# Cross attention: row maximum in bank-sized parts, and a new order of work in the four engine lists of a step

## The reference

```python
kvx = jnp.einsum('bsi,oi->bso', cond, w_kv_x)          # cond: (16, 1601, 256)
kx, vx = jnp.split(kvx, 2, axis=-1)                    # 8 groups of 128
kx = _ln(kx.reshape(b, sc, g, d), kxln_w, kxln_b)      # layer norm of each key
xout = _gqa(qx, kx, vx)                                # softmax(q k / sqrt(128)) v
cat = jnp.concatenate([core, xout], axis=-1)
catq = _div_clamp_fp8(cat, proj_smooth)                # rounding to fp8
```

## Time and profile before

| | before |
|---|---|
| median of 3 runs | 2706.87 us |
| profiled execution | 2704.8 us |
| its span, first to last instruction | 2703.0 us |
| TensorE busy | 2299.4 us (85%) |
| VectorE busy | 2032.5 us (75%) |
| ScalarE busy | 1556.2 us (58%) |
| GpSimd busy | 1472.4 us (54%) |
| mean granted TensorE clock | 0.937 |

### The profile page before, as it was taken

How to read it: one execution, slowest core, us unless ns; L and a number is a source line. 1 busy time by engine, 2 the same in 40 slices (tenths; PEclk the granted TensorE clock), 3 DMA queues, 4 the chain that set the end, 5 groups by cost and what they waited for, 6 DMA issues and landing times. The chain is left out here.

```text
span 2703.0 us, 49677 instructions
## 1 busy us (share of the span) xinstructions
PE 2299.4 (85%) x18258; PEld 1833.9 (68%) x18258; DVE 2032.5 (75%) x4418; ACT 1556.2 (58%) x3133; POOL 1472.4 (54%) x1529
## 2 busy tenths in 40 slices
PE   2888737999999999999999999999999999675566
PEld 1555525877777878787778777777787877553334
DVE  8988845777878787877877787787878777468763
ACT  5767615666666666666666666666666666321211
POOL 3343366666667666676767666666766654250000
PEclk8887759999999999999999999999999999887778
DMA  2010131000110110011010100111011000073100
GB/s 109 40 47 24 47 131 57 27 32 27 52 33 26 34 47 32 27 39 46 26 33 34 45 27 32 35 44 33 34 33 39 20 9 1 28 264 94 35 12 8
DMA packets 74623, 119.41 MB, mean 44 GB/s; under 512 B 21184, under 2 KB 56592, under 8 KB 73360
## 3 DMA queue, kind: packets, MB, share of 16 engines
q1 hardware_dynamic: 74384, 116.23, 12.6%
HBM read 94.20 MB, written 22.02 MB: 43 GB/s over the span
## 5 line engine op out<-in xcount | busy, mean ns | idle before, releaser
L75 PE MATMUL x_kc<-x_wk,x_ctxT 128*128 128x256 f16 x4992 | 624.0, 274 | 49.5 <-POOL x_ctxT L1015 36.7
L1037 POOL TENSOR_TENSOR x_kT<-x_kf,x_kT 128x512 f16<-128x512 f32 (+1 forms) x448 | 625.5, 1396 | 37.3
L75 PE MATMUL x_ox<-x_ctxp,x_pt 128*128 128x256 f16 x4992 | 619.0, 273 | 0.0
L1035 POOL TENSOR_SCALAR x_kT<-x_kf 128x512 f16<-128x512 f32 (+1 forms) x448 | 297.8, 665 | 588.5 <-ACT x_kf L1107 586.7
L75 PEld LDWEIGHTS x_kc<-x_wk,x_ctxT 128*128 128x128 f16 x4992 | 482.0, 98 | 129.4 <-issue 36.8
L75 PEld LDWEIGHTS x_ox<-x_ctxp,x_pt 128*128 128x128 f16 x4992 | 486.2, 98 | 70.4 <-DVE x_on L1368 14.3
L1095 ACT ACTIVATE x_kraw<-x_kc 128x512 f32<-128x512 f32 (+1 forms) x448 | 254.3, 568 | 427.9 <-PE x_kc L75 215.8
L1303 DVE TENSOR_REDUCE x_ss<-x_sq 128x4 f32<-128x512 f32 (+1 forms) x448 | 283.1, 642 | 239.4 <-ACT x_sq L1099 237.9
L1360 DVE TENSOR_TENSOR x_pt<-x_tp,x_pt 128x512 f16<-128x512 f32 (+1 forms) x512 | 297.7, 585 | 108.4 <-ACT x_pt L1134 103.6
L1107 ACT ACTIVATE x_kf<-x_tp,x_hv 128x512 f32<-128x512 f32 (+1 forms) x448 | 330.7, 755 | 75.6 <-PE x_tp L1186 72.2
L1221 PE MATMUL x_tp<-x_ident,x_pb 128*128 128x128 f32 x1664 | 257.2, 274 | 52.7 <-ACT x_pb L1128 50.5
(11 more groups left out here) (238 smaller groups left out, 3077.7 us busy)
## 6 DMA issues: line engine op xcount, KB each, us to landing
x_stage<-in_ctxT SPq DMA_DIRECT2D x32, 800.5 KB, 4.3
x_stage<-in_ctx SPq DMA_DIRECT2D x16, 896.0 KB, 5.1
x_stage<-in_ctx SPq DMA_DIRECT2D x16, 640.0 KB
scr_q<-a_qxT SPq DMA_DIRECT2D x8, 1024.0 KB, 4.1
x_qs<-scr_q SPq DMA_DIRECT2D x16, 512.0 KB, 5.4
scr_x<-x_catx SPq DMA_DIRECT2D x8, 512.0 KB, 2.6
f_area<-in_wprojT SPq DMA_DIRECT2D x4, 1024.0 KB, 10.5
f_cat<-scr_core SPq DMA_DIRECT2D x8, 512.0 KB, 7.5
```

Source lines behind the costliest of these rows:

```text
L75: last = pe.matmul(out, lhs[i], rhs[j], start=start and n == 0, stop=stop and n == len(parts) - 1)
L1035: gp.tensor_scalar(dst[0], src, 1.0, 0.0, ALU.mult, ALU.add).then_inc(khi_ready, 1)
L1037: gp.tensor_tensor(dst[1], src, dst[0], ALU.subtract).then_inc(kT_ready, 1)
```

## The change

`("max", A)` no longer waits for all of `s3`. TensorE raises a semaphore (`sc_parts`) after each of the three banks; VectorE reduces banks 0 and 1 as they come, then the remainder, combines these three, and reduces bank 2 last. The four lists of a step are written anew: the three given ones, and GpSimd's as `POOL_ORDER`. Projections run in the order 1, 0, 2, 5, 6, 3, 4 (`K_ORDER`, taken from TensorE's list) and their semaphore counts follow it. `norm` waits for all seven copies of its step. SP's and GpSimd's waits on the scores count three times as high. The arithmetic stays the same, apart from the maximum being taken in parts.

```diff
-        ORDER = [("m", 0), ("sr", 0), ("sc", 0), ("pv", -1, 0), ("pv", -1, 1), ("tr", 0), ("oa", -2), ("m", 1),
-                 ("tr", 1), ("ob", -2), ("pt", 0, 0), ("pv", -1, 2), ("pt", 0, 1), ("m", 2), ("tr", 2), ("pt", 0, 2),
-                 ("pv", -1, 3), ("pt", 0, 3), ("m", 3), ("tr", 3), ("sr", 1), ("sc", 1), ("m", 4), ("pv", 0, 0),
-                 ("tr", 4), ("oa", -1), ("pv", 0, 1), ("m", 5), ("tr", 5), ("ob", -1), ("tr", 6), ("pv", 0, 2),
-                 ("pt", 1, 0), ("m", 6), ("pt", 1, 1), ("pt", 1, 2), ("pv", 0, 3), ("pt", 1, 3)]
...
+        ORDER = [("m", 1), ("pv", -1, 0), ("sr", 0), ("sc", 0), ("tr", 0), ("tr", 1), ("oa", -2), ("pv", -1, 1),
+                 ("sr", 1), ("m", 0), ("pv", -1, 2), ("ob", -2), ("pt", 0, 0), ("pv", -1, 3), ("m", 2), ("tr", 2),
+                 ("pt", 0, 1), ("pt", 0, 2), ("m", 5), ("tr", 3), ("sc", 1), ("tr", 4), ("m", 6), ("pt", 0, 3),
+                 ("tr", 5), ("pv", 0, 0), ("oa", -1), ("m", 3), ("pv", 0, 1), ("pt", 1, 0), ("m", 4), ("pt", 1, 1),
+                 ("ob", -1), ("pv", 0, 2), ("pv", 0, 3), ("pt", 1, 2), ("tr", 6), ("pt", 1, 3)]
+
+        ACT_ORDER = [("sr", 0), ("tr", 0), ("m", 1), ("oa", -2), ("tr", 1), ("exp", 0), ("m", 0), ("pt", 0, 0),
+                     ("sr", 1), ("m", 2), ("tr", 2), ("pt", 0, 1), ("pt", 0, 2), ("tr", 3), ("m", 5), ("tr", 4),
+                     ("pt", 0, 3), ("m", 6), ("exp", 1), ("tr", 5), ("oa", -1), ("m", 3), ("pt", 1, 0), ("m", 4),
+                     ("pt", 1, 1), ("tr", 6), ("pt", 1, 2), ("pt", 1, 3)]
+
+        DVE_ORDER = [("norm", 0), ("quant", 0), ("max", 0), ("oa", -2), ("m", 1), ("norm", 1), ("ob", -2), ("m", 0),
+                     ("quant", 1), ("quant", 2), ("pt", 0, 0), ("m", 2), ("on", -1), ("pt", 0, 1), ("pt", 0, 2),
+                     ("max", 1), ("quant", 3), ("m", 5), ("pt", 0, 3), ("oa", -1), ("m", 6), ("pt", 1, 0), ("m", 3),
+                     ("ob", -1), ("m", 4), ("pt", 1, 1), ("rs", 0), ("rs", 1), ("rs", 2), ("rs", 3), ("on", 0),
+                     ("rs", 4), ("pt", 1, 2), ("rs", 5), ("rs", 6), ("quant", 4), ("rs", 7), ("rs", 8), ("pt", 1, 3),
                      ("rs", 9), ("rs", 10)]
+
+        POOL_ORDER = [("k", 0), ("k", 1), ("c", 0), ("k", 2), ("c", 1), ("c", 2), ("k", 3), ("c", 3), ("k", 4),
+                      ("k", 5), ("k", 6)]
+
+        K_ORDER = [o[1] for o in ORDER if o[0] == "m"]
...
-                    ins.then_inc(sc_done if kind == "sc" else sr_filled, 1)
+                        if kind == "sc":
+                            ins.then_inc(sc_parts, 1)
+                    if kind == "sr":
+                        ins.then_inc(sr_filled, 1)
...
-                v.wait_ge(kraw_ready, 4 + JK * KU + (A_CH // 2 if half == 0 else KU))
+                v.wait_ge(kraw_ready, 4 + (JK + 1) * KU)
...
-                    v.wait_ge(sc_done, J * 2 + A_ + 1)
-                    v.tensor_reduce(m1[:, A_:A_ + 1], s3[:], X, ALU.max).then_inc(m_chain, 1)
+                    for n in range(2):
+                        v.wait_ge(sc_parts, (J * 2 + A_) * 3 + n + 1)
+                        v.tensor_reduce(m2[:, A_, n:n + 1], s3[:, n * 512:(n + 1) * 512], X, ALU.max).then_inc(m_chain, 1)
                     v.wait_ge(sr_ready, J * 2 + A_ + 1)
-                    v.tensor_reduce(m2[:, A_:A_ + 1], srem[:, A_], X, ALU.max).then_inc(m_chain, 1)
-                    v.wait_ge(m_chain, (J * 2 + A_ + 1) * 2)
-                    v.tensor_scalar(negm[:, A_:A_ + 1], m1[:, A_:A_ + 1], m2[:, A_:A_ + 1], -SOFTMAX_SCALE, ALU.max,
+                    v.tensor_reduce(m2[:, A_, 2:3], srem[:, A_], X, ALU.max).then_inc(m_chain, 1)
+                    v.wait_ge(m_chain, (J * 2 + A_) * 5 + 3)
+                    v.tensor_scalar(m2[:, A_, 3:4], m2[:, A_, 0:1], m2[:, A_, 1:2], m2[:, A_, 2:3], ALU.max, ALU.max
+                                    ).then_inc(m_chain, 1)
+                    v.wait_ge(sc_parts, (J * 2 + A_ + 1) * 3)
+                    v.tensor_reduce(m1[:, A_:A_ + 1], s3[:, 1024:1536], X, ALU.max).then_inc(m_chain, 1)
+                    v.wait_ge(m_chain, (J * 2 + A_ + 1) * 5)
+                    v.tensor_scalar(negm[:, A_:A_ + 1], m1[:, A_:A_ + 1], m2[:, A_, 3:4], -SOFTMAX_SCALE, ALU.max,
                                     ALU.mult).then_inc(negm_ready, 1)
```

More of the change, by code:

```diff
@@ L781, in cross_attend @@
         m1 = sb("m1", [P, 2])
-        m2 = sb("m2", [P, 2])
+        m2 = sb("m2", [P, 2, 4])
         negm = sb("negm", [P, 2])
@@ L814, in cross_attend @@
         sr_ready = sem("sr_ready")
-        sc_done = sem("sc_done")
+        sc_parts = sem("sc_parts")
         m_chain = sem("m_chain")
@@ L838, in last @@
             return isinstance(t, int) and t == TILES - 1
-        ORDER = [("m", 0), ("sr", 0), ("sc", 0), ("pv", -1, 0), ("pv", -1, 1), ("tr", 0), ("oa", -2), ("m", 1),
[4 rows of a table removed]
-        ACT_ORDER = [("sr", 0), ("m", 0), ("tr", 0), ("oa", -2), ("exp", 0), ("m", 1), ("tr", 1), ("pt", 0, 0),
[3 rows of a table removed]
-        DVE_ORDER = [("norm", 0), ("max", 0), ("oa", -2), ("norm", 1), ("m", 0), ("m", 1), ("ob", -2), ("quant", 0),
[4 rows of a table removed]
+        ORDER = [("m", 1), ("pv", -1, 0), ("sr", 0), ("sc", 0), ("tr", 0), ("tr", 1), ("oa", -2), ("pv", -1, 1),
[4 rows of a table added]
+        ACT_ORDER = [("sr", 0), ("tr", 0), ("m", 1), ("oa", -2), ("tr", 1), ("exp", 0), ("m", 0), ("pt", 0, 0),
[3 rows of a table added]
+        DVE_ORDER = [("norm", 0), ("quant", 0), ("max", 0), ("oa", -2), ("m", 1), ("norm", 1), ("ob", -2), ("m", 0),
[4 rows of a table added]
                      ("rs", 9), ("rs", 10)]
+        POOL_ORDER = [("k", 0), ("k", 1), ("c", 0), ("k", 2), ("c", 1), ("c", 2), ("k", 3), ("c", 3), ("k", 4),
+                      ("k", 5), ("k", 6)]
+        K_ORDER = [o[1] for o in ORDER if o[0] == "m"]
         TP_KINDS = ("sr", "tr", "pt", "oa", "ob")
@@ L971, in tile @@
                         if not first(t):
-                            sp.wait_ge(sc_done, t * 16)
+                            sp.wait_ge(sc_parts, t * 48)
                         load_q(t, 1)
@@ L976, in tile @@
                     if j == 5 and not last(t):
-                        sp.wait_ge(sc_done, t * 16 + 8)
+                        sp.wait_ge(sc_parts, t * 48 + 24)
                         load_q(t + 1, 0)
@@ L1030, in split_unit @@
                 if i == 0 and not (isinstance(JK, int) and JK < 2):
-                    gp.wait_ge(sc_done, (JK - 1) * 2)
+                    gp.wait_ge(sc_parts, (JK - 1) * 6)
                 met()
@@ L1049, in tile @@
                     slot = (j // SPB + 1) % 2 if rows else (j // SPB) % 2
[L1050 to L1054, removed]
+                    for kind, n in POOL_ORDER:
+                        if kind == "k" and exists(t, j, ("tr", n)):
+                            split_unit(JK, j + 1, n)
+                        if kind == "c" and convert_here:
                             if n == 0 and not (first(t) and j < 2):
@@ L1086, in raw @@
             def raw(t, JK, jk, i):
-                u = JK * KU + i
+                at = K_ORDER.index(i)
+                u = JK * KU + at
                 n = len(chunks(i)) * 2 * P
@@ L1098, in raw @@
                     act.wait_ge(ss_ready, u - 1)
-                act.activation(sq[:, (jk * KU + i) % 2, 0:n], src, ACT.Square).then_inc(sq_ready, 1)
+                act.activation(sq[:, (jk * KU + at) % 2, 0:n], src, ACT.Square).then_inc(sq_ready, 1)
             def keep_k(JK, jk, i, bank):
@@ L1138, in part @@
                     act.activation(onT[:, 0], tp[:, tp_bank(j, o), 0:C], ACT.Copy).then_inc(onThi_ready, 1)
-            for i in range(KU):
+            for i in K_ORDER:
                 raw(0, 0, 0, i)
@@ L1143, in _ @@
                 keep_k(0, 0, i, i % TPB)
-                raw(0, 1, 1, i)
+                raw(0, 1, 1, K_ORDER[i])
             def tile(t):
@@ L1164, in project_k @@
             def project_k(JK, jk, i):
-                u = JK * KU + i
-                if i == 0 and jk % SPB == 0:
+                at = K_ORDER.index(i)
+                u = JK * KU + at
+                if at == 0 and jk % SPB == 0:
                     pe.wait_ge(ctxT_ready, 8 * (JK // SPB + 1) if isinstance(JK, int) else JK * 2 + 8)
@@ L1258, in _ @@
                 transpose_k(0, i, i % TPB)
-                project_k(1, 1, i)
+                project_k(1, 1, K_ORDER[i])
             def tile(t):
@@ L1301, in square_sum @@
                 n = len(chunks(i)) * 2
-                v.wait_ge(sq_ready, JK * KU + i + 1)
-                v.tensor_reduce(ss[:, 4 * i:4 * i + n], sq[:, (jk * KU + i) % 2, 0:n * D].rearrange("p (n d) -> p n d", d=D),
+                at = K_ORDER.index(i)
+                v.wait_ge(sq_ready, JK * KU + at + 1)
+                v.tensor_reduce(ss[:, 4 * i:4 * i + n], sq[:, (jk * KU + at) % 2, 0:n * D].rearrange("p (n d) -> p n d", d=D),
                                 X, ALU.add).then_inc(ss_ready, 1)
```

## The result

The changed kernel takes 2606.7 us (median of 4 runs, 2605.1 to 2609.5) against 2705.9 beside it: 0.9635 of the time, 95% interval 0.9624 to 0.9647, 99 us faster. The forecast was 66 us (2641), with a range down to 2606. So the forecast had two thirds of the gain. The result lies at the very edge of the range, outside the own range of 2620 to 2668, and the range reaches that far only because it takes in the first rival's price (2608). The time is that rival's, but its reason did not come.

What follows compares the result with a forecast made beforehand. TensorE was taken as the bound. A full step of 27.93 + 0.65 + 0.25 = 28.83 us against 29.90 saves 66 us over 62 steps: 2704.8 - 66 + 2.1 = 2641 us, range 2606 to 2688.

Steps and rivals of the forecast that it cites:

- own range: Range of the forecast's own case without the rivals, 2620 to 2668 us, given a chance of 0.61.
- first rival: The walk closes nearly wholly, as end-of-step and quantising stalls hide each other: 28.3 us a step, 99 us saved, 2608; chance 0.16.
- The bound and the floor: Cross attention: TensorE is the bound, with 27.9 us of work a step without stall against 29.90 taken.
- Change 1: VectorE's maximum in parts: 0.43 us more a group, at most 0.2 us a step gained, counted as 0.
- The walk: New lists followed through a step without quantisation: ScalarE margins 0.05 to 1.5 us, old TensorE waits gone.
- What is late next: VectorE's end of step: norm 0 done at 32.6, when tr0 wants it; no margin, 0.25 us a step charged.
- Quantising steps: Quant 2 stalls pt(0,2), quant 4 stalls tr0: 2.6 us for four steps, 0.65 a step.
- The last two steps: Last two steps of the stage, priced together with the prologue at plus or minus 2 us.
- The second: Rival: margins of 0.05 to 0.15 fail and one more VectorE-GpSimd pair collides; 29.6 a step, 19 us saved, 2688; chance 0.14.
- The third: Rival, slower: VectorE's rs, on and norm 0 wait for late GpSimd; two collisions, 1.6 us, give 2726; chance 0.09.

Runs made afterwards that it cites:

- order-only kernel: The changed kernel with its new lists, but the maximum again as one reduce of 1536 waiting for all three banks: 2616.6 us, 0.9672 of the kernel before.
- GpSimd's old order: The changed kernel with GpSimd's conversions again behind k2, k3, k4 and k5 as before: 2610.2 us, 0.9647 of the kernel before.
- the filler: The changed kernel with one more VectorE instruction ahead of norm 0, a reduce of 512 elements of an unused buffer: 2637.2 us, 0.9750 of the kernel before.
- the quantising operations moved: The changed kernel with quant 1 and 2 behind the second maximum, quant 3 ahead of oa(-1), quant 4 behind m6: 2589.6 us, 0.9571 of the kernel before.

## Why the prediction was right, and where its size was off

*The bound and the floor: right.* 27.9 us a step without stall was worked out from starts of matmuls before (its terms add up to 27.87, the sum goes on with 27.93), and 27.94 is what a step without a wait takes now.

*Change 1: right in length, and wrong on what the parts bring.* The added 0.43 us is 0.44. "So the order brings nearly all of the gain and the parts 0.2 us a step at most [...] I count 0": net of their cost the parts bring 0.15 us a step, 10 us in all, shown by the order-only kernel. This is no part of the 33 us between forecast and result, as the walk that gave the sum was that of the kernel with the parts.

*The walk: right.* Every margin on ScalarE held in the middle of the stage, down to 0.05; the waits for the exponential, the subtraction and kT went. Margins were not eaten by scatter, as durations repeat to some 0.01 us.

*What is late next: right place, wrong price.* "Margin none: I charge 0.25 a step" is the term that was mis-sized most. The margin was 0.02 us and held in every step without quantisation before it, so the charge was 0, and steps foreseen at 28.1 to 28.3 take 27.94. It held by little: k6 ran ahead of most of rs4 to rs10, but held up one rs operation in each step (L1334, 0.41 in place of 0.19, at 1006.83 and again at 1034.78). There most of it costs nothing: the subtraction behind it needs a copy of ScalarE that ends at 1035.04, and starts at 1035.11. 0.25 x 62 = 15.5 us of the 33 missing.

*Quantising steps: right places, over-sized.* Both stalls came where they were put. Forecast 2.6 for four steps (2.2 at the least), measured 0.84 + 0.99 = 1.83, 0.46 a step in place of 0.65: 12 us. The reason is in the earlier trace rows: 1.26 and 1.59 are not the operations' own times but hold a wait for GpSimd. The shortest of the same instruction was at hand in the view by line, 0.43 and 1.22:

```profile
L1394 DVE TENSOR_SCALAR x_yf<-x_eb x16: 428/1262/1264, 604.7 to 2353.8; 128x1024 bf16<-128x1024 bf16 x16
L1400 DVE TENSOR_TENSOR x_catx<-x_y,x_yf x16: 1216/1590/1594, 612.9 to 2355.5; 128x1024 f16<-128x1024 f32 x16
```

(Shortest, median and longest in ns.) Quant 4 has its shortest time in the new order. Quant 2 does not: it meets GpSimd there too and takes 0.72, so its shortest would have priced its stall some 0.3 us too low; with GpSimd's old order it takes 0.43 and the stall is 0.29 shorter.

*The last two steps.* They were given plus or minus 2 us and brought 5.0: from the 63rd step's first remainder to the last matmuls of "ob", 2295.35 to 2351.99 before and 2201.03 to 2252.65 after. 15.5 + 12 + 5 make up the 33 us between forecast and result. The order-only kernel takes 52.75 there (2210.36 to 2263.11), so 3.9 of the 5.0 come with the lists; which move in them does it is open.

*The rivals.* The first had the price but not the mechanism: the stalls did not hide each other, they were smaller; that the time fell inside the range is owed to a price that stood there for another reason. The second, failing margins, did not come. The third, collisions at the end of VectorE's step, came as one short collision a step that fits into the slack. Its place is the right one: 0.48 us more there cost 0.46 with the filler, and longer collisions at the same place cost time with the quantising operations moved and with GpSimd's old order.

## What to carry to other kernels

Where one engine is near its floor, walk the lists once with start-to-start distances and write down each margin; a reordering is worth what its walk closes, and a split of a reduce only what its consumer is really waiting for at that moment. When another engine can hold an operation up, take its own time from the shortest of its rows, and add a collision only where the new order has one: a median row carries a collision of the old order along. Small repeated work (here once in four steps) belongs where its engine waits for another, and long operations that hold another engine up belong apart from each other.

## What the runs showed of the hardware

VectorE operations with two inputs in SBUF, and some with one, hold up GpSimd and are held up by it until the running instruction ends: besides the rows above, norm 1 of 2304 elements takes 2.92 us in place of 2.60 (2.55 at its shortest) when a GpSimd instruction has started just ahead of it, and GpSimd's subtraction 3.33 in place of 1.16, ending 1.00 behind norm 1. The tensor_scalar operations of quantisation are of this kind too (quant 2: 0.43, 0.72 or 1.26 us). The Trainium skill, SBUF — State Buffer, section Who interferes with whom, states that VectorE and GpSimd contend for one shared pair of ports by an exclusive lock, for VectorE instructions with two SBUF inputs and for tensor_scalar in its two-port modes. The trace agrees.

```profile
1042.20 2.92 DVE L1344 TENSOR_TENSOR x_kn<-x_kraw,x_rk 128x2304 f32<-128x2304 f32 x1
```

```profile
1042.09 0.62 POOL L1041 TENSOR_SCALAR x_kT<-x_kf 128x512 f16<-128x512 f32 x1
1042.79 3.33 POOL L1043 TENSOR_TENSOR x_kT<-x_kf,x_kT 128x512 f16<-128x512 f32 x1
```

The combination of three maxima, one input and two per-partition scalars, on 128x1, took 0.27 us in each of 128 cases in the changed kernel, in 35 of them while one GpSimd instruction ran from before its start to after its end; no collision of it is seen.
